# Rounding the Gelu outputs in two halves on GpSimd, in a fused attention and feed-forward kernel

## The reference

```python
def _bitlinear(x, w):
    rms = jax.lax.rsqrt(jnp.maximum(jnp.mean(w * w), EPS))
    w_quant = jnp.clip(jnp.round(w * rms), -1.0, 1.0) / rms
    scale = 127.0 / jnp.maximum(jnp.max(jnp.abs(x), axis=-1, keepdims=True), EPS)
    x_quant = jnp.clip(jnp.round(x * scale), -128.0, 127.0) / scale
    return jnp.einsum('bsd,fd->bsf', x_quant, w_quant)
...
x = x + _L0_conv_ref(_ln_c(x), L0_conv_fc1_w, L0_conv_fc2_w, L0_conv_sa_w)
t = _to_tokens(x)
h = jax.nn.gelu(_bitlinear(_ln_t(t), w1), approximate=False)
t = t + _bitlinear(h, w2)
```

## Time and profile before

| | |
|---|---|
| median of 3 runs | 332.18 us (331.9 to 332.73) |
| the profiled execution | 332.48 us, of which the span of the trace is 330.7 us |
| busy, share of the span: PE | 294.7 us, 89% |
| DVE | 278.5 us, 84% |
| ACT | 222.2 us, 67% |
| POOL | 142.5 us, 43% |
| granted TensorE clock, after the start-up | full |

### The profile page before, as it was taken

One profiled execution on the slowest core, in us unless ns is written; L12 is line 12 of the kernel. 1 busy time (PEld: TensorE's weight loads), 2 busy tenths in 40 slices (PEclk: granted clock), 3 DMA queues, 4 the chain that ended last, 5 costly groups with the idle time before them and its releaser, 6 DMA issues. The chain is left out here.

```text
span 330.7 us, 6659 instructions
## 1 busy us (share of the span) xinstructions
PE 294.7 (89%) x2230; PEld 176.0 (53%) x2230; DVE 278.5 (84%) x667; ACT 222.2 (67%) x493; POOL 142.5 (43%) x193
## 2 busy tenths in 40 slices
PE   2458666699999999999999999999999999999994
PEld 2345534646555565646564646464746565555551
DVE  0757989789899989998999899998899899989840
ACT  2286397477775877587658666866686668666662
POOL 7405347223733374337342834184327433653330
PEclk9755679659999999999999999999999999999999
DMA  4999600000001220113010401040104010101103
GB/s 127 318 389 414 182 1 2 0 0 2 4 0 50 61 85 1 50 41 103 2 50 17 128 0 51 0 146 0 50 1 146 2 49 1 50 2 48 48 3 95
DMA packets 21449, 22.44 MB, mean 68 GB/s; under 512 B 1384, under 2 KB 18792, under 8 KB 20904
## 3 DMA queue, kind: packets, MB, share of 16 engines
q1 hardware_dynamic: 19752, 20.98, 19.1%
q10 hardware_dynamic: 1664, 1.05, 1.1%
HBM read 15.73 MB, written 6.29 MB: 67 GB/s over the span
## 5 line engine op out<-in xcount | busy, mean ns | idle before, releaser
L1125 PE MATMUL ps_o<-w2T,hq 128*128 128x512 f16 x384 | 92.6, 380 | 0.0
L1102 PE MATMUL ps_h<-w1T,xq 128*128 128x512 f16 x296 | 74.6, 389 | 0.8 <-ACT xq L491 0.8
L448 POOL TENSOR_SCALAR w_room<-w_room,q 128x2048 f32<-128x2048 f32 x24 | 47.4, 1974 | 62.7 <-DVE q L822 62.7
L491 ACT ACTIVATE w_room<-ps_h,s 128x512 f32<-128x512 f32 x74 | 50.2, 688 | 15.8 <-PE ps_h L1102 13.5
L809 DVE TENSOR_REDUCE amax<-w_room 128x1 f32<-128x1024 f32 x48 | 57.1, 1207 | 1.4 <-ACT w_room L491 1.4
L1125 PEld LDWEIGHTS ps_o<-w2T,hq 128*128 128x128 f16 x384 | 35.0, 98 | 36.9 <-ACT hq L491 3.5
L491 ACT ACTIVATE hq<-ps_t 128x512 f16<-128x512 f16 x96 | 51.4, 608 | 2.4 <-PE ps_t L1115 2.4
L1102 PEld LDWEIGHTS ps_h<-w1T,xq 128*128 128x128 f16 x296 | 27.3, 99 | 32.4 <-issue 2.6
L491 ACT ACTIVATE junk_m<-front 128x192 bf16<-128x192 f32 x64 | 20.5, 327 | 25.2 <-DVE pooled L724 25.0
L782 DVE SCALAR_TENSOR_TENSOR t<-pv,sg,xt 128x512 f32<-128x512 f32 x24 | 31.9, 1328 | 2.7 <-DVE res L832 0.5
L443 POOL TENSOR_SCALAR cen<-cen,q 128x512 f32<-128x512 f32 x24 | 16.6, 691 | 35.9 <-DVE q L804 35.9
(11 more groups left out here) (126 smaller groups left out, 491.6 us busy)
## 6 DMA issues: line engine op xcount, KB each, us to landing
x_in<-in_x SPq DMA_DIRECT2D x16, 384.0 KB, 5.2
out<-w_room SPq DMA_DIRECT2D x16, 384.0 KB, 2.6
w_room<-in_L_ffn_w SPq DMA_DIRECT2D x4, 1024.0 KB, 9.3
w_raw<-in_L_ffn_w SPq DMA_DIRECT2D x4, 1024.0 KB, 12.3
x_in<-in_x ACTq DMA_DIRECT2D x2, 384.0 KB, 3.9
fc_raw<-in_L_conv_fc_w ACTq DMA_DIRECT2D x2, 128.0 KB, 4.2
taps_rev<-in_L_conv_sa_w SPq DMA_DIRECT2D x2, 0.2 KB
taps_rev<-in_L_conv_sa_w SPq DMA_DIRECT2D x2, 0.3 KB
```

The source lines that it names most:

```text
L448: pool.tensor_scalar(c[:, :], c[:, :], q2[tile.par][:, 0:1], MAGIC, ALU.mult, ALU.add).then_inc(g_rounded, 1)
L491: act.activation(out_ap, in_ap, func, **more).then_inc(signal, 1)
L1102: last = pe.matmul(banks[b], xq[tile.pair.par][:, tile.s, k, :], w1T[:, k, b * 512:(b + 1) * 512], start=(k == 0), stop=(k == NC - 1))
L1125: last = pe.matmul(ps_o[:, :], hq[tile.par][:, k, :], w2T[:, k, :], start=(k == 0), stop=(k == NF - 1))
```

## The change

`round_g` runs over `g` in two instructions of 1024 columns, each with a signal of its own, so that `g_rounded` now counts two per tile. DVE's wait before it overwrites `q2` counts both halves of the tile before (`tile.at(2, -2)` for `tile.at(1, -1)`), so it waits for the same thing as earlier. PE's `turn_hq` waits for the first half ahead of its first 8 transposes and for the second ahead of the other 8.

```diff
             def round_g(tile):
                 wait(pool, q2_ready, tile.at(1, 1))
-                c = g[tile.par]
-                pool.tensor_scalar(c[:, :], c[:, :], q2[tile.par][:, 0:1], MAGIC, ALU.mult, ALU.add).then_inc(g_rounded, 1)
+                for half in range(2):
+                    part = g[tile.par][:, half * F // 2:(half + 1) * F // 2]
+                    pool.tensor_scalar(part, part, q2[tile.par][:, 0:1], MAGIC, ALU.mult, ALU.add).then_inc(g_rounded, 1)
...
-                wait(dve, g_rounded, tile.at(1, -1))
+                wait(dve, g_rounded, tile.at(2, -2))
                 dve.reciprocal(q2[tile.par][:, :], lim127[:, :]).then_inc(q2_ready, 1)
...
             def turn_hq(tile, last_in=None):
 
-                wait(pe, g_rounded, tile.at(1, 1))
                 q = low_halves(g[tile.par][:, :])
                 for i in range(2):
+                    wait(pe, g_rounded, tile.at(2, i + 1))
                     wait(pe, hq_ready, tile.at(4, 2 * i - 2))
```

## The result

The change took 329.14 us (median of 6 runs, 328.77 to 330.63) where the kernel before took 332.23 (6 runs, 331.9 to 333.12) beside it: ratio 0.9911, interval 0.9887 to 0.9936. The same kernel measured once more, with the experiments, gave 330.61 (5 runs, 329.86 to 330.93) against 332.14, ratio 0.9955, interval 0.9942 to 0.9968. So the change is faster, by 1.5 to 3 us, and part of what follows is about why one kernel has two results, whose intervals don't meet.

A forecast was written before the change was run, and what follows sets the result against it. The period was taken as a loop of POOL's stretch from L448 to L419, then DVE's list, with PE following at little slack. Six times (0.26 - 0.84 + 0.35) gave -1.4 us, from 332.18 to 330.8 us, range 328.8 to 333.0.

The forecast's parts named there:

- (A): First rounding of a period: POOL's second half starts before DVE's L782, so DVE loses 0.26 us.
- (B): Second rounding of a period: DVE's L782 gets in between POOL's two halves, changing DVE by -0.84 us.
- PE's early start: PE's transposes hardly wait for the rounding, so having the first half earlier gains PE nothing.
- Length of a half: POOL's rounding of 1024 columns takes 1.12 us; both halves end at +2.23, 0.26 later than now.
- (C): Third rounding of a period: L782 holds POOL's L424, so L419 and DVE's L798 come 0.35 us later (0 to 0.4).
- From there to the next `q2` DVE goes from one instruction to the next: After L798, DVE's list runs without waiting until the next period's `q2`.
- The sum: Three roundings per period, six times with effect: 6 x (0.26 - 0.84 + 0.35) = -1.4 us.
- Later roundings lie beside an uninterrupted PE: Roundings after the six counted occurrences run beside a PE that does not stop; no term in the sum.
- 1 (DVE wins the race in (A)): At a period's first rounding L782 goes before the second half, -0.60 us there; total 329.5 us, chance 0.25.
- 2 (the door stays shut): POOL keeps the port through both halves, L782 ends 0.26 us later in (A) and (B); 337.4 us, chance 0.10.
- 3: (B)'s gain meets PE or ACT at the end of DVE's list and cancels against (A) + (C); 332.2 us, chance 0.10.

The follow-up runs named there:

- experiment 1: Every tile rounded in two halves as in the change, but PE waits for both halves: 330.51 us, ratio 0.9958; compared with the change measured again, 330.61 us.
- experiment 6: Kernel before with only the very first tile's rounding cut in halves: 331.63 us, ratio 0.9985.
- cuts_for_the_door: Kernel before with a period's first rounding cut at column 1152, second at 640, third whole, very first tile in halves: 330.93 us, ratio 0.9959.
- change_again: The change itself, unaltered, measured again on another chip beside the kernel before: 330.61 us, ratio 0.9955.
- split_pe_waits_whole: The change's halves for every tile, but PE waits for both before its first transpose: 330.51 us, ratio 0.9958.
- experiment 5: Kernel before with only a period's first rounding cut, at 1152: 330.20 us; then cuts at 1152, 640 and none, very first tile in halves: 330.93 us.
- best_cuts_sums_first: Kernel before with first rounding cut at 1152, second at 1024, third whole, and ACT's later channel sums before its copy out: 328.76 us, ratio 0.9898.
- split_second_only: Kernel before with only a period's second rounding cut in halves, very first tile whole: 330.19 us, ratio 0.9945.
- split_third_only: Kernel before with only a period's third rounding cut in halves: 332.71 us, ratio 1.0023.
- sums_first_alone: Kernel before, no cut, with ACT's two later channel sums placed ahead of a tile's copy out: 329.67 us, ratio 0.9933.

## Why the prediction was right, and where not

Forecast 330.8 (328.8 to 333.0), faster likeliest; measured 329.14 and 330.61. The sign and the mechanism of (A) and (B) held. The size of a period's gain held by luck: two errors cancel in it. The total did not: the first measurement gained 3.1 us and not 1.4, and most of the surplus lies in the start, which the sum had left out; the second gained 1.5, with less than the forecast in a period.

**PE's early start: right in the periods, not at the end.** "So an earlier first half buys PE nothing" held for the periods (experiment 1). In the tail it is worth about 0.5 us, since there PE comes to two tiles before both of their halves are done.

**Length of a half: right.** 1.12 us free, the second started at +1.10, both done at +2.22.

**(A), +0.26: right.** 1.60 to 1.61 us in each period, +0.25 alone. Beside (B) it turned out free.

**(B), -0.84: right in the duration, wrong in what it is worth.** `t` took 0.96, as written (+0.70 to +1.66). But "From there to the next `q2` DVE goes from one instruction to the next" is a statement on the trace of before. ACT's third sum had been ready early enough by less than the gain, and nothing in the list of waits showed it, because a wait with slack isn't listed. The slack could have been read: ACT's sum ends at 215.52 + 0.18 = 215.70 and DVE's L760 starts at 215.76. I looked for PE and ACT only as rivals and gave them 0.10.

**(C), +0.35: the mechanism was wrong.** I had L424 held by `t`. I had asked of each POOL call what DVE does to it, and of `t` what the halves do to it, but not of the small DVE calls ahead of `t`: `sg` is held by the second half, `t` comes later, and with a lead of 0.03 in place of the 0.18 that I had counted on it doesn't hold L424. Nothing of what follows from that came: L424 took 0.19 and not 0.6, `cen` 0.91 and not 0.49, and DVE's wait for the root stayed at 0.93 instead of growing to 1.7. Measured +0.16 (+0.14 alone), inside what I had bounded (0 to 0.4).

**The sum.** Written: 0.26 - 0.84 + 0.35 = -0.23 a period. Measured: -0.26 in the first result, -0.09 mostly in the second. By steps of the list in the first: (A) +0.25, (B) -0.85, waiting for ACT +0.29, the collision of the split with `v` 0.08 smaller, and +0.16 in the stretch, together -0.23. The agreement is a coincidence of (C) mis-sized by 0.2 and 0.2 lost to ACT, for which the sum had no term.

**Start and tail.** "Later roundings lie beside an uninterrupted PE" held: the doors brought two of the last four intervals 0.85 us each, and the next one was 1.4 longer, so that the four together shrank by 0.15. The first tile's door was not priced: -0.5 us. The spans differ by 3.7, which the starts of the roundings place as follows: 0.8 us before the first one, 0.85 from it to the second (8.49 for 9.34), 0.7 in the first period (34.20 for 34.90), 1.1 in the five that follow (167.7 for 168.8), 0.15 in the tail. So almost two thirds of the difference of these two profiles lie ahead of the steady periods, of which the forecast spoke, and the two executions began differently (experiment 6).

**Rivals.** 1 (DVE wins the race in (A)) did not happen, but with a first piece 0.1 us longer (1152 columns) it does. 2 (the door stays shut) did not happen with 1024 columns; in *cuts_for_the_door* it did, four times of six, and not because POOL keeps the port through both calls but because DVE came as the first piece ended. 3 happened in part.

**What differs between the two measurements.** In the profiles (span 327.0 and 328.1) 0.46 us lie before the first rounding, 0.17 in the first period, and 0.46 in the five that follow: 33.65 to 33.68 four times and 33.48 once, where the first has 33.50 four times and 33.68 once. One of the long ones is the same in both, a period whose `t` in (B) came at +1.06. The other three are a slower kind that the first profile doesn't have. From *change_again*:

```profile
179.97 0.65 DVE L761 CAST stat_split<-ch_stat 128x6 bf16<-128x6 f32 x1 [0.23 <-ACT junk_p L492]
...
179.82 0.76 POOL L431 TENSOR_SCALAR v<-xt,minus_mean,rs 128x512 f32<-128x512 f32 x1
```

Here the first of the four small instructions comes 0.15 after `v` and is held, at 0.65 us; in the faster kind (rows above) it comes 0.11 after and goes through, and the second, held for 0.45, ends earlier: 0.2 us a period for 0.04 us of start. Read to the nanosecond, in the three profiles that cut every tile in halves it goes through at 0.112 to 0.133 us behind `v` and is held at 0.136 to 0.145. I have shown that the two kinds exist and what each does, not why the border lies there, nor why one execution falls on this side of it more often.

The start is the other candidate. Both profiles began in the way in which the first cut pays (`t` at +0.47). *split_pe_waits_whole*, which cuts the same columns, began in the other, and from its first rounding to the first steady period it is 43.85 us, where these two have 42.69 and 42.86. The times of the change's own six runs spread over 1.9 us, which fits such a mix, but the start is known only for the profiled ones.

## What to carry to other kernels

When an edit makes one engine earlier, read the slack of everything that engine takes from others at the end of its list, not only the waits that are listed: here 0.86 us gained became 0.26. Where GpSimd and VectorE run next to each other, an instruction's start decides more than its length, so look at each pair of starts within 0.1 us or so, the small instructions too, and measure cut points rather than choose halves. A new wait is not a loss by itself: if the waiting engine was early at a meeting point anyway, it can let the other one through. And measure a kernel more than once before you explain its time: here one kernel gave 0.9911 and 0.9955.

## What the runs showed of the hardware

- **A door between two GpSimd calls.** A VectorE `t` held by one call gets in before the next, already issued one: held to +1.12, done at +1.66. It did so in (B) in all five steady periods of six kernels with a cut at 1024 there; in a seventh, *best_cuts_sums_first*, once it came too late for the door. The held GpSimd half gets 0.43 us longer. The Trainium skill, "SBUF — State Buffer", section "SBUF: two separate sides", has the shared ports as a lock that is kept by whoever starts first, for the whole instruction. Both 1.61 in (A) and 0.96 in (B) agree with it. Row L424 of the changed kernel doesn't, taken by its recorded start: it came 0.03 after `t` and was not held. Nor do, though the prediction says that no row speaks against the rule: there `t` came 0.08 after L424, while that ran, and took its free 0.75. Which of the two took the ports first can't be told from the records at such distances.
- **The race is closer than two decimals.** Starts 0.79 us apart gave 1.97 and 0.75 us (experiment 5), and 0.133 us passed where 0.136 was held.
- **Small VectorE instructions are held too.** `sg` with 3 columns takes 0.32 for 0.16, a cast with 6 columns 0.62 or 0.65 for 0.16, each beside a GpSimd call of 0.76 us or more that had started first.
- **TensorE's clock in the start.** In the stretch that ends about where the first rounding starts (before, then the change) the granted clock was 0.50, the level of 1.2 GHz throughout, and 0.86, mostly 2.4 GHz:

```profile
66.00:72.00 6.00, 6.00 (x36) 3.16 (x33) 5.11 (x12) 4.61 (x7) 0.00 (x0) 0.50 0.00 0
```

```profile
66.00:72.00 6.00, 5.76 (x39) 2.70 (x36) 5.35 (x15) 5.44 (x11) 0.70 (x1) 0.86 0.00 0
```

It isn't the change: of the 14 profiles in the table above, six have 0.50 there (before, *split_pe_waits_whole*, *split_second_only* and three more), and the other eight, among them *split_third_only* and *sums_first_alone*, which leave the first tile whole, 0.78 to 0.89. The six are exactly those in which `t` came 1.09 after the first rounding's start, and the eight those with 0.47 (experiment 6). Which of the two brings the other about wasn't tested. It is one profile of each, so how often an execution has which was not measured. The 0.8 us ahead of the first rounding don't follow from it alone: that rounding starts at 71.85 to 72.12 us in the six and at 71.25 to 72.02 in the eight.
